# Six units of expert work ahead of a 128-step recurrence, and three in place of two between its steps

## The chip, the cores and the metric

The kernel runs on all 8 cores of one Trainium2 chip. Each core takes 2048 of the 16384 tokens and computes them from end to end; there is no exchange between cores. The time of a run is the device time of the slowest core, in microseconds (us). The profile is that of the slowest core of one execution.

## The reference

The input is normalised over its 1024 features. Two branches read the result, and both are added to the input.

```python
xn = _layernorm(x)
# branch 1: a recurrence over the tokens of a sequence
u = xn @ Wi.T + bi ; sp = xn @ Ws.T + bs        # 128 states
state = tanh(state @ A.T + u_t @ B.T) + sp_t
y_t = state @ C.T ; out1 = ys @ Wo.T + bo
# branch 2: 8 experts, the best 2 of each token, weighted
w = softmax over the top 2 of xn @ router_weight, zero elsewhere
gate, up = xn @ gate_up_proj (1024 -> 1024 each)
act = (clip(up, -7, 7) + 1) * min(gate, 7) * sigmoid(1.702 * gate)
out2 = sum_e w[e] * (act[e] @ down_proj[e])
y = x + out1 + out2
```

## The kernel before, in words

The program is written out in Python as five lists of instructions, one for each engine, in the order of the Python code. Nothing reorders them. An instruction waits on semaphore counts given where it is written; VectorE's and ScalarE's instructions also wait for the one before them on their own engine.

A core's work has four stages.

1. Normalisation of 17 blocks of 128 tokens (16 own, one of the tokens before), their transposition to `xn_fm`, the projections `u` and `sp`, the term of the recurrence that doesn't depend on the state (`Dt`), and the routing weights.
2. The recurrence, called the chain here. The 2048 tokens are cut into 64 pieces of 32; each piece starts 96 tokens early from a zero state, so that the chain has `NSTEP` = 96 + 32 = 128 steps, and each step handles one token of all 64 pieces. Step s is a matmul of `sAT` (L693, 64 columns) that adds A times the last state to a bank of PSUM, and a tanh on ScalarE (L702) that writes the new state. For each pair of steps, two matmuls of the identity (L680) first place `Dt` in the banks `pb4` and `pb5`. Steps 0 to 95 write the small buffer `gw`; steps 96 to 127 write `G`, a strided tile of which every 32nd column is written at a time. A step's matmul waits for the tanh of the step before.
3. Output of branch 1: u_bf (L712) on VectorE, a matmul by C (L721), 64 matmuls by Wo and the down bias (L736, L741) that ScalarE moves to `acc` (L746), and on VectorE 32 multiplications of expert 0's activations by their routing weights (L755).
4. The experts: down projection of expert 0 (L866, added to `acc` at L882), then gate, up and down of experts 1 to 7, and the output.

The gate and up projections of expert 0 do not wait for the chain, and are woven into it. They are 32 tiles (8 slices of 128 features, 4 of 512 tokens each), and `gu_tile_gen` writes one tile: 8 matmuls of 512 columns for gate (L277), 8 for up (L287), and then the elementwise work. The generator pauses after every second matmul, so a tile has 8 units of 2 matmuls, and all of expert 0 has 256. The elementwise work of a tile comes when the generator is resumed after its eighth unit. `pump(n)` writes the next n units, and goes from one tile to the next. For a tile of expert 0 the elementwise work is seven instructions on VectorE (casts of gate and up from PSUM, L311 and L313; L318, L321, L324; L335 and L338), and one sigmoid on ScalarE (L326), which stands in ScalarE's list between two tanhs. The sigmoid needs L318, and L335 needs the sigmoid. Gate and up use two PSUM banks each in turn, so that a tile's matmuls wait for the casts of the tile two before. After the chain, `pump_all` writes whatever units are left.

Of the kernel before, what the change touches and what calls it, by code (L numbers as in the profile page):

```python
# [35 lines left out]
def build_nc(debug=False, upto="full", ntc_run=None, skip_big=False):  # L36
# [48 lines left out]
    with ExitStack() as _es:  # L85
# [73 lines left out]
        if True:  # L159
# [48 lines left out]
            try:  # L208
# [139 lines left out]
                def pump(n):  # L348
                    k = 0
                    while k < n:  # L350
                        if pump_cur[0] is None:
                            if not pump_q:
                                return
                            ei_, fc_, stt_ = pump_q[0]
                            if stt_ > ready_st[0]:
                                return
                            pump_q.pop(0)
                            pump_cur[0] = gu_tile_gen(ei_, fc_, stt_, weighted=False)
                        try:
                            next(pump_cur[0])  # L360
                            k += 1
                        except StopIteration:
                            pump_cur[0] = None
# [300 lines left out]

                if PH < 2: raise _Done()
                ch_act = {}
                for s in range(NSTEP):
                    pump(2)
                    b = s % 2
                    if b == 0:  # L670
                        for k in range(2):
                            sk = s + k
                            if sk >= NSTEP:
                                break
                            wl = []
                            if k == 0:
                                wl = [("s_ve", ve_d_all),
                                      ("s_sc", ch_act[s - 1] if s > 0 else cnt["s_sc"])]
                            te(lambda e, sk=sk, bk=pb[4 + sk % 2]:
                               e.matmul(bk[:, 0:NCH], sI16[:],  # L680
                                        Dt[:, WOFF + sk:WOFF + sk + SSTR:LCH],
                                        start=True, stop=False, skip_group_check=True),
                               wait=wl, inc=False)
                    if s == 0:
                        rhs = gz[:]
                    elif s <= WCH:
                        rhs = gw[:, ((s - 1) % 2) * NCH:((s - 1) % 2) * NCH + NCH]
                    else:
                        t0 = s - 1 - WCH
                        rhs = G[:, t0:t0 + SSTR:LCH]  # L690
                    wl = [("s_sc", ch_act[s - 1])] if s > 0 else []
                    mv = te(lambda e, b=b, rhs=rhs:
                            e.matmul(pb[4 + b][:, 0:NCH], sAT[:], rhs,  # L693
                                     start=False, stop=True, skip_group_check=True),
                            wait=wl)
                    if s < WCH:
                        dst = gw[:, (s % 2) * NCH:(s % 2) * NCH + NCH]
                    else:
                        t0 = s - WCH
                        dst = G[:, t0:t0 + SSTR:LCH]  # L700
                    ch_act[s] = sc(lambda e, b=b, dst=dst:
                                   e.activation(dst, pb[4 + b][:, 0:NCH], ACT.Tanh),  # L702
                                   wait=[("s_te", mv)])
# [310 lines left out]
```

How the kernel before makes its waits and increments, by code:

```python
                    def op(e, fn=fn, w=w, v=v, sem_name=sem_name):  # L176
                        for sn, val in w:
                            e.wait_ge(sems[sn], val)
                        ins = fn(e)
                        if v is not None:
                            ins.then_inc(sems[sem_name], 1)
# [19 lines left out]
                def op(e, dst=dst, src=src, w=w, sem_name=sem_name):  # L201
                    for sn, val in w:
                        e.wait_ge(sems[sn], val)
                    e.dma_start(dst, src).then_inc(sems[sem_name], 16)
# [706 lines left out]
            def fin(e):  # L911
                if fin_o0:
                    e.wait_ge(s_ou0, fin_o0)
                if fin_o1:
                    e.wait_ge(s_ou1, fin_o1)
```

## Time and profile before

| | us |
|---|---|
| median of 8 runs | 1665.14 |
| lowest and highest of them | 1662.87, 1714.15 |
| the profiled execution's own time | 1663.5 |
| its span, slowest core (core 1) | 1662.0 |
| spans of the 8 cores | 1657.9 to 1662.0 |
| first gate matmul of expert 0 | 156.91 |
| last tanh of the chain begins | 316.49 |
| first u_bf addition (L712) begins | 319.84 |

Times inside the execution are counted from the span's start. The chain and expert 0's gate and up take from 156.91 to 316.49, that is, about a tenth of the span; the expert work of stage 4 fills nearly all the rest after 359.61.

### The profile page before, as it was taken

The page shows a single profiled execution, that of the slowest core. Times are in us where ns is not written, and L with a number is a line of the kernel's source. Part 1 is how long each engine was busy: PE and PEld are TensorE (multiplying, and loading weights), DVE is VectorE, ACT ScalarE, POOL GpSimd, SP SyncE. Part 2 cuts the span into 40 slices and gives each one's busy share as a digit, 9 for nine tenths or more (in the row PEclk, how much of TensorE's full clock was granted, in tenths as well). Part 3 has the DMA queues.
Part 4 walks back from the last instruction along what each step waited for, and adds up shares of the span by engine and source line. Part 5 has one row for each costly group of instructions (what it writes and reads, how often), then busy time and mean ns, then how long its engine had stood idle before and what let it go on. Part 6 is the DMA issues. An engine that isn't in the chain of part 4 may idle for free.

```text
span 1662.0 us, 25899 instructions; the slowest of 8 cores (1657.9 to 1662.0 us)
## 1 busy us (share of the span) xinstructions
PE 1485.9 (89%) x6998; PEld 669.4 (40%) x6998; DVE 903.0 (54%) x2133; ACT 560.4 (34%) x1013; POOL 120.3 (7%) x230
## 2 busy tenths in 40 slices
PE   0445888899999999999999999999999999999973
PEld 0221444324444444444444444444444444444432
DVE  4554666623566456635664466446644665366543
ACT  3442333440554045404550355025512551155200
POOL 2000000000000000000000000000000000000011
PEclk9766999869999999999999999999999999999995
DMA  5400111102222222221222222212221222222158
GB/s 145 112 26 1 27 26 27 26 7 39 33 39 40 39 31 39 39 45 26 38 40 45 33 39 39 41 30 39 39 45 27 39 39 44 33 39 39 20 113 211
DMA packets 36314, 74.66 MB, mean 45 GB/s; under 512 B 4864, under 2 KB 4864, under 8 KB 36176
## 3 DMA queue, kind: packets, MB, share of 16 engines
q0 software_dynamic: 31424, 55.71, 22.3%
q1 hardware_dynamic: 4752, 17.30, 3.1%
q8 instruction: 63, 1.03, 0.3%
q14 instruction: 75, 0.61, 0.1%
HBM read 120.10 MB, written 8.39 MB: 77 GB/s over the span
## 4 chain that ended last, share of the span: by engine, by line
PE 82%; DVE 6%; DMA 5%; ACT 3%; issue 3%; DVEq 0%; ACTq 0%; POOL 0%; POOLq 0%; SPq 0%
PE pb L287 27%; PE pb L866 26%; PE pb L277 25%; DMA y<-otm 1%; DMA xres<-xm 1%; DVE etu L313 1%; PE pb L736 1%; PE pb L741 1%; ACT et L326 1%; PE pb L479 1%; DVE acc L882 1%; DVE otm L800 1%; PE pb L693 1%; DVE etg L318 1%; PE pb L680 1%
## 5 line engine op out<-in xcount | busy, mean ns | idle before, releaser
L277 PE MATMUL pb<-xn_fm,wgu 128*128 128x512 bf16 x2048 | 496.3, 383 | 1.6 <-ACT wbc L656 1.0
L287 PE MATMUL pb<-xn_fm,wgu 128*128 128x512 bf16 x2048 | 490.4, 380 | 0.0
L866 PE MATMUL pb<-act_w,wdb_ 128*128 128x512 bf16 x2048 | 450.2, 382 | 6.8 <-DVE acc L882 5.9
L882 DVE TENSOR_TENSOR acc<-acc,pb 128x512 bf16<-128x512 bf16 x256 | 176.1, 688 | 276.5 <-PE pb L866 273.9
L866 PEld LDWEIGHTS pb<-act_w,wdb_ 128*128 128x128 bf16 x2048 | 200.9, 98 | 252.9 <-issue 16.3
L277 PEld LDWEIGHTS pb<-xn_fm,wgu 128*128 128x128 bf16 x2048 | 197.8, 99 | 239.3 <-issue 17.2
L287 PEld LDWEIGHTS pb<-xn_fm,wgu 128*128 128x128 bf16 x2048 | 197.6, 98 | 229.8 <-issue 3.3
L307 ACT CAST etu<-pb 128x512 bf16<-128x512 f32 x224 | 131.3, 586 | 256.0 <-PE pb L287 256.0
L326 ACT ACTIVATE et<-etg 128x512 bf16<-128x512 bf16 x256 | 161.1, 629 | 66.4 <-DVE etg L318 32.4
L305 ACT CAST etg<-pb 128x512 bf16<-128x512 f32 x224 | 131.3, 586 | 91.1 <-PE pb L277 90.3
L321 DVE TENSOR_SCALAR etu<-etu,sbu 128x512 bf16<-128x512 bf16 x256 | 91.9, 359 | 110.5 <-ACT etu L307 104.9
L839 ACT CAST wbc<-pb 128x512 bf16<-128x512 f32 x28 | 16.4, 586 | 394.8 <-PE pb L833 392.8
L318 DVE TENSOR_SCALAR etg<-etg,sbg 128x512 bf16<-128x512 bf16 x256 | 90.4, 353 | 81.7 <-DVE act_w L338 38.2
L331 DVE TENSOR_TENSOR et2w<-et,wbc 128x512 bf16<-128x512 bf16 x224 | 95.2, 425 | 54.5 <-DVE etu L324 53.1
L338 DVE TENSOR_TENSOR act_w<-etu,et2w 128x512 bf16<-128x512 bf16 x256 | 108.8, 425 | 26.7
L333 DVE TENSOR_TENSOR et2w<-etg,et2w 128x512 bf16<-128x512 bf16 x224 | 95.3, 426 | 23.3
L204 POOL DMA_DIRECT2D wgu<-Wg x64 | 33.9, 529 | 778.3 <-PE pb L287 546.5
L324 DVE TENSOR_SCALAR etu<-etu 128x512 bf16<-128x512 bf16 x256 | 75.4, 295 | 27.2
L204 POOL DMA_DIRECT2D wdb_<-Wd x64 | 33.8, 528 | 442.2 <-PE pb L866 398.0
L204 POOL DMA_DIRECT2D wgu<-Wu x64 | 34.3, 537 | 235.6 <-DMA wgu<-Wg 214.5
L702 ACT ACTIVATE gw<-pb 128x64 bf16<-128x64 f32 x96 | 21.5, 224 | 57.8 <-PE pb L693 54.4
L313 DVE CAST etu<-pb 128x512 bf16<-128x512 f32 x32 | 22.1, 692 | 25.8 <-PE pb L693 25.8
(105 smaller groups left out, 515.7 us busy)
## 6 DMA issues: line engine op xcount, KB each, us to landing
wgu<-Wg POOLq DMA_DIRECT2D x64, 256.0 KB, 3.5
wgu<-Wu POOLq DMA_DIRECT2D x64, 256.0 KB, 3.6
wdb_<-Wd POOLq DMA_DIRECT2D x64, 256.0 KB, 3.5
xln<-xm SPq DMA_DIRECT2D x16, 512.0 KB, 4.1
y<-otm SPq DMA_DIRECT2D x16, 512.0 KB, 5.7
xres<-xm POOLq DMA_DIRECT2D x16, 256.0 KB, 6.7
xln<-xw SPq DMA_DIRECT2D x1, 512.0 KB, 5.4
sWiT<-WiT POOLq DMA_DIRECT2D x1, 256.0 KB, 6.6
```

Of the source, the lines that this page charges most:

```text
L204: e.dma_start(dst, src).then_inc(sems[sem_name], 16)
L277: e.matmul(bg_[:, 0:STW], wgu[:, 2 * par, dc, :], rhs, start=(dc == 0), stop=(dc == NDC - 1)),
L287: e.matmul(bu2[:, 0:STW], wgu[:, 2 * par + 1, dc, :], rhs, start=(dc == 0), stop=(dc == NDC - 1)),
L305: cg = sc(lambda e, tg=tg, bg_=bg_: e.copy(tg, bg_[:, 0:STW]), wait=[("s_te", mg)])
L307: cu = sc(lambda e, tu=tu, bu2=bu2: e.copy(tu, bu2[:, 0:STW]), wait=[("s_te", mu2)])
L318: e.tensor_scalar(t1, tg, gbias, LIMIT, ALU.add, ALU.min),
L326: e.activation(t2, t1, ACT.Sigmoid, scale=ALPHA),
L331: e.tensor_mul(t2w, t2, wbs),
L333: ve(lambda e, t3=t3, t1=t1, t2w=t2w: e.tensor_mul(t3, t1, t2w))
L338: e.tensor_mul(act_w[:, fc, stt * STW:(stt + 1) * STW], t5_, t3))
L866: e.matmul(bk[:, 0:STW], wdb_[:, par, ic, :], act_w[:, ic, stt * STW:(stt + 1) * STW], start=(ic == 0), stop=(ic == NDC - 1), skip_group_c ...
L882: e.tensor_add(acc[:, fc, stt * STW:(stt + 1) * STW], acc[:, fc, stt * STW:(stt + 1) * STW], bk[:, 0:STW]),
```

## The change

Six units of expert 0 are written ahead of step 0, and each step is preceded by three units in place of two.

```diff
                 ch_act = {}
+                pump(6)
                 for s in range(NSTEP):
-                    pump(2)
+                    pump(3)
                     b = s % 2
```

Before, 128 steps of 2 units made the 256 units. Now 6 + 3 x 83 = 255 units stand ahead of step 83, the last one is written by step 83's call, and steps 84 to 127 have no expert work among them. All lines below the change are one number higher in the new kernel: L680, L693, L702, L712, L736, L866 become L681, L694, L703, L713, L737, L867.

The first place is the start of the chain on TensorE. In these rows `pb_43` and `pb_44` are the two gate banks, `pb_45` and `pb_46` the two up banks, `pb_47` and `pb_48` the two banks of the chain. Before:

```order
L650 MATMUL pb_46<-w_fmb,ssel 128x512
L277 MATMUL pb_43<-xn_fm,wgu 128x512 x4
L680 MATMUL pb_47<-Dt,sI 128x64
L680 MATMUL pb_48<-Dt,sI 128x64
L693 MATMUL pb_47<-gz,sAT 128x64
L277 MATMUL pb_43<-xn_fm,wgu 128x512 x4
L693 MATMUL pb_48<-gw,sAT 128x64
L287 MATMUL pb_45<-xn_fm,wgu 128x512 x4
```

And now:

```order
L650 MATMUL pb_46<-w_fmb,ssel 128x512
L277 MATMUL pb_43<-xn_fm,wgu 128x512 x8
L287 MATMUL pb_45<-xn_fm,wgu 128x512 x8
L277 MATMUL pb_44<-xn_fm,wgu 128x512 x2
L681 MATMUL pb_47<-Dt,sI 128x64
L681 MATMUL pb_48<-Dt,sI 128x64
L694 MATMUL pb_47<-gz,sAT 128x64
L277 MATMUL pb_44<-xn_fm,wgu 128x512 x6
L694 MATMUL pb_48<-gw,sAT 128x64
L287 MATMUL pb_46<-xn_fm,wgu 128x512 x6
```

The whole first tile and a unit of the second now stand ahead of step 0, and six matmuls of 512 columns stand between two chain matmuls.

The second place is ScalarE's list between two sigmoids, in the first part of the chain. Before, a sigmoid stands after every four tanhs:

```order
L326 ACTIVATE et2<-etg 128x512
L702 ACTIVATE gw<-pb4_47 128x64
L702 ACTIVATE gw<-pb5_48 128x64
L702 ACTIVATE gw<-pb4_47 128x64
L702 ACTIVATE gw<-pb5_48 128x64
L326 ACTIVATE et2<-etg 128x512
```

And now:

```order
L326 ACTIVATE et2<-etg 128x512
L703 ACTIVATE gw<-pb5_48 128x64
L703 ACTIVATE gw<-pb4_47 128x64
L703 ACTIVATE gw<-pb5_48 128x64
L326 ACTIVATE et2<-etg 128x512
L703 ACTIVATE gw<-pb4_47 128x64
L703 ACTIVATE gw<-pb5_48 128x64
L326 ACTIVATE et2<-etg 128x512
```

Three, three and two tanhs stand between sigmoids now, over and over.

The third place is on TensorE where the expert work ends. Before, it ends with the chain:

```order
L693 MATMUL pb4_47<-G,sAT 128x64
L287 MATMUL pb3_46<-xn_fm,wgu 128x512 x4
L693 MATMUL pb5_48<-G,sAT 128x64
L721 MATMUL pb4_47<-u_bf,sCT 128x512
```

And now, at steps 83 to 85:

```order
L287 MATMUL pb3_46<-xn_fm,wgu 128x512 x2
L694 MATMUL pb5_48<-gw,sAT 128x64
L681 MATMUL pb4_47<-Dt,sI16 128x64
L681 MATMUL pb5_48<-Dt,sI16 128x64
L694 MATMUL pb4_47<-gw,sAT 128x64
L694 MATMUL pb5_48<-gw,sAT 128x64
```

After the last unit, only chain matmuls of 64 columns follow, up to step 127.

## Rows read from the trace of the kernel before

**Rows 1.** The groups of tanhs: count, busy us, mean ns, idle before and releaser.
```profile
L702 ACT ACTIVATE gw<-pb 128x64 bf16<-128x64 f32 x96 | 21.5, 224 | 57.8 <-PE pb L693 54.4
L702 ACT ACTIVATE G<-pb 128x64 bf16<-128x64 f32 x32 | 14.5, 452 | 15.5 <-PE pb L693 14.3
```

**Rows 2.** Stretches: us, each engine's busy us (count), granted clock, DMA share, GB/s.
```profile
160.00:162.00 2.00, 2.00 (x7) 0.77 (x6) 0.69 (x1) 0.22 (x1) 0.00 (x0) 0.51 0.00 0
324.00:358.00 34.00, 33.75 (x63) 6.31 (x63) 11.95 (x29) 20.90 (x31) 0.00 (x0) 0.50 0.00 0
110.00:120.00 10.00, 2.73 (x32) 2.14 (x32) 6.38 (x23) 4.05 (x8) 0.00 (x0) 0.54 0.00 1
160.00:270.00 110.00, 99.11 (x544) 47.83 (x543) 71.86 (x155) 34.03 (x112) 5.28 (x10) 0.99 0.16 25
```

**Rows 3.** Waits from 157 to 317: total us, times, longest.
```profile
ACT et L326 <- DVE etg L318: 31.6, 31, 1.4
PE pb L693 <- ACT gw L702: 11.4, 23, 0.8
```

**Rows 4.** Timeline of one tile's loop: start, length, engine, line, idle before.
```profile
202.38 0.69 DVE L313 CAST etu<-pb 128x512 bf16<-128x512 f32 x1 [0.69 <-PE pb L693]
203.25 0.35 DVE L318 TENSOR_SCALAR etg<-etg,sbg 128x512 bf16<-128x512 bf16 x1 [0.18 <-DVE etu L313]
203.69 0.63 ACT L326 ACTIVATE et<-etg 128x512 bf16<-128x512 bf16 x1 [1.06 <-DVE etg L318]
204.47 0.22 ACT L702 ACTIVATE gw<-pb 128x64 bf16<-128x64 f32 x1
204.84 0.19 PE L693 MATMUL pb<-gw,sAT 128*128 128x64 bf16 x1 [0.49 <-ACT gw L702]
204.96 1.02 PE L287 MATMUL pb<-xn_fm,wgu 128*128 128x512 bf16 x4
205.12 0.22 ACT L702 ACTIVATE gw<-pb 128x64 bf16<-128x64 f32 x1 [0.43 <-PE pb L693]
205.23 0.43 DVE L338 TENSOR_TENSOR act_w<-etu,et2w 128x512 bf16<-128x512 bf16 x1
205.82 0.38 PE L680 MATMUL pb<-Dt,sI 128*128 128x64 bf16 x2
205.83 0.69 DVE L311 CAST etg<-pb 128x512 bf16<-128x512 f32 x1 [0.17 <-DVE act_w L338]
206.03 0.21 PE L693 MATMUL pb<-gw,sAT 128*128 128x64 bf16 x1
206.07 1.02 PE L287 MATMUL pb<-xn_fm,wgu 128*128 128x512 bf16 x4
207.20 0.69 DVE L313 CAST etu<-pb 128x512 bf16<-128x512 f32 x1 [0.69 <-PE pb L693]
208.07 0.35 DVE L318 TENSOR_SCALAR etg<-etg,sbg 128x512 bf16<-128x512 bf16 x1 [0.18 <-DVE etu L313]
```

**Rows 5.** Timeline of the chain's first step.
```profile
156.91 1.86 PE L277 MATMUL pb<-xn_fm,wgu 128*128 128x512 bf16 x4 [1.03 <-ACT wbc L656]
158.80 0.23 PE L693 MATMUL pb<-gz,sAT 128*128 128x64 bf16 x1
159.13 0.22 ACT L702 ACTIVATE gw<-pb 128x64 bf16<-128x64 f32 x1 [2.57 <-PE pb L693]
```

**Rows 6.** Timeline in the last quarter: tanh to matmul to tanh.
```profile
308.22 0.45 ACT L702 ACTIVATE G<-pb 128x64 bf16<-128x64 f32 x1
308.81 0.27 PE L693 MATMUL pb<-G,sAT 128*128 128x64 bf16 x1 [0.76 <-ACT G L702]
309.18 0.45 ACT L702 ACTIVATE G<-pb 128x64 bf16<-128x64 f32 x1 [0.51 <-PE pb L693]
```

**Rows 7.** Timeline at the chain's end: the last tanh and the first addition after it.
```profile
316.49 0.45 ACT L702 ACTIVATE G<-pb 128x64 bf16<-128x64 f32 x1 [0.52 <-PE pb L693]
319.84 2.02 DVE L712 TENSOR_TENSOR u_bf<-G,SPb 128x512 bf16<-128x512 bf16 x4 [0.17 <-DVE act_w L338]
```

## The prediction, made before the changed kernel ran

> **What bounds the kernel now.** I read the page's 40 slices first: TensorE is busy through the chain and through the experts, so only one stretch can be moved by this change, that from the first gate matmul at 156.91 [rows 5] to the first u_bf addition at 319.84 [rows 7]. All later stages start from that addition. So the forecast is the new time of that addition, less 319.84.
>
> TensorE's busy share in that stretch looks like a bound (99.1 of 110 us), but busy time of pipelined matmuls overstates it. The waits say otherwise: the sigmoid waited 31 times for VectorE's L318, 31.6 us in all, and a chain matmul waited 23 times for its tanh in the first 96 steps [rows 3]. So I followed one tile in the timeline [rows 4]. L318 begins at 203.25, the sigmoid that it releases at 203.69, the tanh queued behind the sigmoid at 204.47, the chain matmul that waits for that tanh at 204.84. Only then does TensorE go on: four matmuls of 512 columns from 204.96, the pair of L680 at 205.82, the next chain matmul at 206.03, four more from 206.07. The last four end the up projection of the tile; VectorE's cast of it starts at 207.20, and L318 of the next tile at 208.07. This is a closed loop of 208.07 - 203.25 = 4.82 us a tile: 1.59 us from L318 to the chain matmul, 2.36 from there to the up cast, 0.87 from cast to L318. Neither engine fills it. Free of waits, TensorE would need per tile 16 matmuls of 0.215 us (four take 205.82 - 204.96 = 0.86), that is 3.44, and for four steps 4 x 0.11 + 2 x 0.21 = 0.86, together 4.3. VectorE needs 205.83 - 203.25 = 2.58 from L318 to the next gate cast, and 0.87 each for the two casts (each is a cast of 0.69 and a gap near 0.18, as from 202.38 to 203.25), together 4.32.
>
> **The first three quarters of the units, faster.** In the new order (the order of the two kernels is in the section on the change) 3 units stand between chain matmuls, so a tile spans 8/3 steps. TensorE's floor falls to 3.44 + 8/3 x 0.11 + 4/3 x 0.21 = 4.0 us; VectorE's stays at 4.32. The loop depends on how many units of tile n+1 come ahead of the chain matmul that is held by tile n's sigmoid. Before, these were always 4, and 4 were left. Now it is 4, then 6, then 5, in turn, as the 3, 3, 2 tanhs between sigmoids tell. With 4 ahead the loop stays as it was, 4 units left and about 4.82. With 5 or 6 ahead, 3 or 2 units are left: 1.59 + 0.12 + 3 x 0.43 + 0.27 = 3.27 us from L318 until the up cast can start (0.27 is the delay from TensorE's end to the cast, 207.20 less 206.07 + 0.86), while VectorE itself is ready for that cast only after 2.58 + 0.87 = 3.45. So there VectorE is the bound and a tile takes 4.32. Mean (4.82 + 2 x 4.32)/3 = 4.49.
>
> The head: the first tile's 16 matmuls now run without a chain step among them. The granted clock was 0.51 up to 162 [rows 2], which is 1.2 GHz, and 512 columns take 0.427 there: four of them lasted 1.86, the last one's drain included [rows 5]. From 156.91 to 161.9 these are 11.7 matmuls, the other 4.3 take 0.9: tile 0 is through at 162.8, and its L318 begins at 162.8 + 0.27 + 0.87 = 164.0. Then 31 loops, 11 of 4.82 and 20 of 4.32, are 139.4 us: the last tile's L318 begins at 303.4. The sigmoid of this tile is written ahead of step 83's tanh, so the matmul of step 84 comes 1.59 later, plus the pair of L680 ahead of it: 305.1. Before, by the same measure, 2 units a step carried the expert work to the end of the chain.
>
> **The last 44 steps, bare.** From step 84 nothing is left to weave in, and a step costs its latency. In the first kind of step (gw) the tanh's start to the next chain matmul is 204.84 - 204.47 = 0.37, the matmul to its tanh 205.12 - 204.84 = 0.28 [rows 4]: 0.65 us, and 0.21 more where a pair of L680 comes in between (205.82 to 206.03): 0.86. For steps that write G the two are 308.81 - 308.22 = 0.59 and 309.18 - 308.81 = 0.37 [rows 6], so 0.96, and 1.17 with a pair; half of this is the tanh itself, 0.452 us against 0.224 [rows 1]. Twelve gw steps: 6 x 0.65 + 6 x 0.86 = 9.1. From step 96 to step 127's matmul: 16 x 0.96 + 15 x 1.17 = 32.9, and 0.37 + 0.45 to the end of its tanh. Sum 42.8 us at full clock.
>
> The clock will not be full. Where TensorE was busy 2.73 of 10 us, the granted clock was 0.54 [rows 2], that is, mostly 1.2 GHz, and in the bare steps TensorE has a matmul of 64 columns or three of them in about 1 us. At that level step 0 had 0.33 from matmul to tanh [rows 5] against 0.28. No row shows the other side, tanh to matmul, or a pair of L680 that has waited, at that level; I take 0.07 us more per step in all, between 0 and 0.15. So 44 x 0.07 = 3.1, and the tail is 45.9 us (42.8 to 49.4). The Trainium skill says in "TensorE: Matmul & The Clock Gate", section "The HAM clock gate", that half rate is the default and that activity releases it; by that rule the tail is at 1.2 GHz throughout. By the page's formulas for a single matmul (section "Single matmul latency") 64 columns would take an estimated 236 ns there and 193 ns at 2.4 GHz, and the tail would grow by 44 x 0.04 = 1.9 us, and by more where a pair precedes; by "no change of clock" it would be 42.8. The trace's step 0 agrees in direction with the page (0.33 against 0.28), and no row here shows a run of bare steps.
>
> **Sum.** End of the last tanh 305.1 + 45.9 = 351.0. VectorE has by then long finished the last tile (before, that tile held the u_bf addition until 319.84, nearly 3 us after the tanh's end at 316.94; this wait of 2.9 us goes and is in the sum), so the addition starts 0.2 later, at 351.2. Against 319.84 that is +31.4 us. The rest costs nothing new: the same output stage and the same experts follow. Weight loads of expert 0 have 4 tiles, 17 to 19 us, per slice for two transfers of 3.5 us each, and those of expert 1 are issued earlier; the L755 multiplications still lie under the output stage, which ran at a clock of 0.50 before [rows 2] and starts from a slow clock again. The profiled execution took 1663.5, so it would take 1694.9; the median before is 1.6 above it, so I expect 1696.5 as a median, 1.9% slower. (A difference of under 0.2% could not be told from none.)
>
> **Rivals.**
>
> A. *The tile loop does not shorten.* If something puts the slow case in every tile (VectorE held by a sigmoid that comes later, say), 31 loops of 4.82 are 149.4, 10.0 us more: +41.4, 1706. For it speaks that the waits [rows 3] are the same every tile; against it, that in two of three tiles fewer units are left behind the held matmul.
>
> B. *Handoffs in the tail are cheap.* If the gaps around a tanh were due to the 512-column matmuls in TensorE's queue, and went away when it is empty, a step would cost its tanh and the matmul's issue: 12 x 0.25 + 32 x 0.48 = 18.4 us in place of 45.9. That alone leaves +3.9. Together with the same gap gone from the slow tile loops (each at VectorE's 4.32, 5.5 us less) the addition would come at 318.2, 1.6 us sooner than before: 1663.5 as a median, on the faster side of nothing. It decides at 44 steps in 14.5 us, 0.33 each, for the tail alone, less than the mean tanh of 0.39 [rows 1]. And the matmul at 204.84 found TensorE idle for 0.49 us [rows 4]: nothing was ahead of it in the queue, and it still came 0.37 after its tanh's start. So there is next to nothing for it.
>
> C. *The clock rises in the output stage.* It stood at 0.50 for 34 us although TensorE was busy 33.75 of them [rows 2]. If the other history brought it to full there, ScalarE's 32 moves, 0.69 and a gap near 0.1 each, would set the pace: 25.3 in place of 34, so +31.4 - 8.7 = +22.7, 1688. The stage begins after a low clock in both kernels, so little speaks for it.
>
> D. *The change leaves the order as it was.* Excluded by the order of instructions, where steps 84 to 127 stand bare.
>
> **How the numbers follow.** Forecast 0.82 (its own range 1692 to 1702, from the tail's 42.8 to 49.4 and 2 us on the loops), A 0.09, C 0.06, B 0.01, other 0.02. The range from 1689 to 1703 leaves out most of A and C. Slower by over 0.2%: all but B and a part of "other", 0.98; within 0.2%: 0.01; faster: 0.01.
>
> **What would show it.** In the profile after: L318 starts of neighbouring tiles 4.3, 4.3 and 4.8 us apart up to about 303; the last gate or up matmul near 302; from there to about 351 TensorE with a low busy share and a clock near 0.5, chain matmuls 0.7 to 0.95 us apart up to step 96 and 1.0 to 1.25 after it; VectorE idle for 45 us; u_bf's addition at 351; the stages behind it shifted as a block by 31. The forecast is wrong if tiles come under 4.2 or all over 4.7 us apart, if tail steps take under 0.9 or over 1.15 us in the mean, or if a stage behind 351 is longer or shorter by over 2 us.

## The result, and the profile after

The changed kernel takes 1694.9 us (median of 11 runs) against 1665.07 (31 runs): a ratio of 1.0182, with a 95% interval of 1.0173 to 1.0191. Some executions of either kernel were several per cent longer, with one half of the chip at a lower granted clock; the medians here count them, all the ratios leave them out. The change makes the kernel 1.8% slower. The profiled execution took 1694.22; its slowest core, core 5, spans 1692.7.

Here is where the chain's stretch begins and ends in each execution, for the slowest core. The two last rows take out that cores reach the chain at slightly different times.

| us | before (core 1) | changed (core 5) |
|---|---|---|
| first gate matmul | 156.91 | 157.69 |
| last tile's L318 | 317.26 | 306.41 |
| last tanh ends | 316.94 | 351.43 |
| first u_bf addition | 319.84 | 351.53 |
| from the first gate matmul to that addition | 162.9 | 193.8 |
| from that addition to the span's end | 1342.2 | 1341.2 |

The loss is the 30.9 us of the second last row. All that follows has kept its length within 1 us. The other cores say the same: over all eight, the stretch of the second last row is 162.9 to 163.2 us before and 193.4 to 193.8 now, and the rest takes 1340.8 in the mean before and 1340.3 now.

In the timeline of the changed kernel the columns are start, length, engine, line, operation, and in brackets the idle time before with its releaser. Here are two tiles in a row, each from one L318 on VectorE to the next, with the lines that matter for them (others between are left out):

```profile
202.58 0.35 DVE L318 TENSOR_SCALAR etg<-etg,sbg 128x512 bf16<-128x512 bf16 x1 [0.18 <-DVE etu L313]
204.27 0.19 PE L694 MATMUL pb<-gw,sAT 128*128 128x64 bf16 x1
206.03 0.69 DVE L313 CAST etu<-pb 128x512 bf16<-128x512 f32 x1 [0.17 <-PE pb L694]
206.90 0.35 DVE L318 TENSOR_SCALAR etg<-etg,sbg 128x512 bf16<-128x512 bf16 x1 [0.17 <-DVE etu L313]
207.34 0.63 ACT L326 ACTIVATE et<-etg 128x512 bf16<-128x512 bf16 x1 [2.56 <-DVE etg L318]
208.12 0.23 ACT L703 ACTIVATE gw<-pb 128x64 bf16<-128x64 f32 x1
208.49 0.19 PE L694 MATMUL pb<-gw,sAT 128*128 128x64 bf16 x1 [1.19 <-ACT gw L703]
208.62 1.46 PE L287 MATMUL pb<-xn_fm,wgu 128*128 128x512 bf16 x6
210.86 0.69 DVE L313 CAST etu<-pb 128x512 bf16<-128x512 f32 x1 [0.69 <-PE pb L287]
211.72 0.35 DVE L318 TENSOR_SCALAR etg<-etg,sbg 128x512 bf16<-128x512 bf16 x1 [0.18 <-DVE etu L313]
```

From 202.58 to 206.90 a tile took 4.32 us, and the up cast at 206.03 began as soon as VectorE was free (0.17, its usual gap). From 206.90 to 211.72 it took 4.82: the chain matmul at 208.49 had waited for the tanh at 208.12, which stood behind the sigmoid at 207.34; it came 1.59 us after L318, as in [rows 4], and the up cast at 210.86 had to wait 0.69 for TensorE. Over the chain the L318s come about 4.31, 4.31 and 4.83 us apart in turn.

The tail, where nothing is woven in, first in gw steps and then in G steps:

```profile
311.09 0.38 PE L681 MATMUL pb<-Dt,sI 128*128 128x64 bf16 x2 [0.47 <-ACT gw L703]
311.30 0.23 PE L694 MATMUL pb<-gw,sAT 128*128 128x64 bf16 x1
311.62 0.23 ACT L703 ACTIVATE gw<-pb 128x64 bf16<-128x64 f32 x1 [0.68 <-PE pb L694]
311.99 0.21 PE L694 MATMUL pb<-gw,sAT 128*128 128x64 bf16 x1 [0.47 <-ACT gw L703]
312.30 0.23 ACT L703 ACTIVATE gw<-pb 128x64 bf16<-128x64 f32 x1 [0.45 <-PE pb L694]
312.67 0.38 PE L681 MATMUL pb<-Dt,sI 128*128 128x64 bf16 x2 [0.47 <-ACT gw L703]
312.88 0.23 PE L694 MATMUL pb<-gw,sAT 128*128 128x64 bf16 x1
...
345.37 0.29 PE L694 MATMUL pb<-G,sAT 128*128 128x64 bf16 x1
345.76 0.45 ACT L703 ACTIVATE G<-pb 128x64 bf16<-128x64 f32 x1 [0.73 <-PE pb L694]
346.35 0.27 PE L694 MATMUL pb<-G,sAT 128*128 128x64 bf16 x1 [0.69 <-ACT G L703]
346.71 0.45 ACT L703 ACTIVATE G<-pb 128x64 bf16<-128x64 f32 x1 [0.51 <-PE pb L694]
347.31 0.38 PE L681 MATMUL pb<-Dt,sI 128*128 128x64 bf16 x2 [0.69 <-ACT G L703]
347.51 0.29 PE L694 MATMUL pb<-G,sAT 128*128 128x64 bf16 x1
```

Two gw steps take 312.88 - 311.30 = 1.58 us, two G steps 347.51 - 345.37 = 2.14. TensorE waits for ScalarE at each step and ScalarE for TensorE. The stretches of the same execution (columns as in [rows 2]) give the clock in the tail and in the output stage, and the waits from 157 to 352 (total us, times, longest) what VectorE does meanwhile:

```profile
320.00:345.00 25.00, 8.64 (x45) 3.96 (x45) 0.00 (x0) 10.74 (x24) 0.00 (x0) 0.50 0.00 1
356.00:389.00 33.00, 32.86 (x62) 6.10 (x61) 11.74 (x28) 20.65 (x30) 0.00 (x0) 0.50 0.00 0
```

```profile
DVE u_bf L713 <- ACT G L703: 42.7, 1, 42.7
```

In the tail the granted clock is 0.50, the lower level of 1.2 GHz, and VectorE stands idle for 42.7 us. And at the head, step 0 shows a wait that was not there before:

```profile
165.48 0.63 ACT L326 ACTIVATE et<-etg 128x512 bf16<-128x512 bf16 x1 [8.15 <-DVE etg L318]
166.26 0.38 PE L681 MATMUL pb<-Dt,sI 128*128 128x64 bf16 x2 [1.77 <-ACT et L326]
166.46 0.21 PE L694 MATMUL pb<-gz,sAT 128*128 128x64 bf16 x1
```

Step 0's first matmul waits for the last ScalarE instruction written so far (`cnt["s_sc"]`). Nine units are written ahead of it now, the six and step 0's own three, so the first tile's elementwise work is too, and that last instruction is the first tile's sigmoid. TensorE idles 1.77 us.

### The profile page after: what moved, and what is told of

It reads as the page before. It is cut to its first block, busy times and chain, and to the rows that moved or that the text cites. A ratio compares the mean times of both kernels' runs of the same rounds, so it can differ in the third digit from the quotient of the medians.

```text
span 1692.7 us, 25899 instructions; the slowest of 8 cores (1687.9 to 1692.7 us)
## 1 busy us (share of the span) xinstructions
PE 1488.9 (88%) x6998; PEld 669.9 (40%) x6998; DVE 903.1 (53%) x2133; ACT 561.4 (33%) x1013; POOL 120.4 (7%) x230
## 4 chain that ended last, share of the span: by engine, by line
PE 83%; DVE 5%; DMA 4%; ACT 4%; issue 3%; DVEq 0%; ACTq 0%; POOL 0%; POOLq 0%; SPq 0%
PE pb L287 26%; PE pb L867 26%; PE pb L277 25%; DMA xres<-xm 2%; PE pb L681 1%; PE pb L737 1%; PE pb L742 1%; DVE etu L313 1%; ACT G L703 1%; PE pb L479 1%; ACT et L326 1%; PE pb L694 1%; DVE acc L883 1%; DVE otm L801 1%; PE pb L491 1%
## 5 line engine op out<-in xcount | busy, mean ns | idle before, releaser
L867 PE MATMUL pb<-act_w,wdb_ 128*128 128x512 bf16 x2048 | 449.7, 382 | 6.8 <-DVE acc L883 5.9
L867 PEld LDWEIGHTS pb<-act_w,wdb_ 128*128 128x128 bf16 x2048 | 200.9, 98 | 252.8 <-issue 16.2
L318 DVE TENSOR_SCALAR etg<-etg,sbg 128x512 bf16<-128x512 bf16 x256 | 90.5, 354 | 81.4 <-DVE act_w L338 38.2
L338 DVE TENSOR_TENSOR act_w<-etu,et2w 128x512 bf16<-128x512 bf16 x256 | 108.8, 425 | 26.7
L204 POOL DMA_DIRECT2D wgu<-Wu x64 | 34.0, 531 | 259.5 <-DMA wgu<-Wg 191.0
L681 PE MATMUL pb<-Dt,sI 128*128 128x64 bf16 x128 | 24.3, 278 | 21.1 <-ACT G L703 10.3
L703 ACT ACTIVATE gw<-pb 128x64 bf16<-128x64 f32 x96 | 21.6, 225 | 55.8 <-PE pb L694 51.3
```

Source lines behind the costliest of these rows:

```text
L204: e.dma_start(dst, src).then_inc(sems[sem_name], 16)
L338: e.tensor_mul(act_w[:, fc, stt * STW:(stt + 1) * STW], t5_, t3))
L867: e.matmul(bk[:, 0:STW], wdb_[:, par, ic, :], act_w[:, ic, stt * STW:(stt + 1) * STW], start=(ic == 0), stop=(ic == NDC - 1), skip_group_c ...
```

## Experiments

The theory T: the change splits the chain into 84 steps paced by the tiles (4.31 us, every third 4.83, for 8/3 steps) and 44 bare steps that cost their handoffs, and the second part is far dearer than what the first gives back. Each time below is a median with its ratio to the kernel before on the same chip; "stretch" is the time from the first gate matmul to the first u_bf addition on the slowest core of the profiled execution (162.9 before, 193.8 changed). Bare steps are those with no expert work among them, and the tail is the run of bare steps at the chain's end.

**Three units, none ahead.**

```diff
-                    pump(2)
+                    pump(3)
```

> Three units before each step, no six ahead: one part of the change alone. Theory T (the loss is the bare tail, priced by its own latency): units end in step 85, so 42 bare steps in place of 44, two gw steps fewer (2 x 0.79 = 1.6 us), and step 0 no longer waits for the first tile's sigmoid (1.1 us in the profile of the changed kernel). Expect about 2.5 us less than the changed kernel: 1692 to 1693, ratio to before 1.0165. Rival R1 (the six units ahead, a head of TensorE work that delays the chain, carry a good part of the loss): then this kernel should be at least 6 us below the changed one, 1689 or less.

Measured: 1691.53 us, ratio 1.0170 (1.0154 to 1.0186); stretch 191.0, which is 2.9 less than the changed kernel's. The number of units a step carries the loss; R1, the head, falls.

**Six units ahead, two a step.**

```diff
+                pump(6)
                 for s in range(NSTEP):
                     pump(2)
```

> Six units ahead, two before each step: the other part alone. Theory T: units end in step 124 and only three steps are bare; the tile loops stay at 4.83 us. The last tile's L318 comes near 316.9 as before, and three bare G steps with their last tanh follow: +1 us (0 to 2), 1666, no difference that this measurement tells well. Rival R1: the head costs by itself, 5 us or more, 1670 and above.

Measured: 1663.83 us, ratio 1.0003 (0.9992 to 1.0014); stretch 162.1. That is 0.9 less than before where I expected 1 more. The tile loops in the gw part are mostly 4.73 to 4.82, a little under the 4.83 of before, which I put down to the pair of L681 standing elsewhere in the tile (not tried); and the addition no longer waits for the last tile. No difference in time, as expected.

**The bare steps first.**

```diff
-                    pump(2)
+                    pump(3 if s >= 42 else 0)
```

> No units before steps 0 to 41, three before each of steps 42 to 127: as many bare steps as with three only (42), but at the chain's start, where each writes gw, while the 32 G steps have expert work among them. Theory T (a bare step costs its handoffs, 0.79 us in the mean for gw and 1.07 for G): the bare part is 42 x 0.79 = 33 us in place of 43, the G steps under expert work add about 0.3 us to each slow tile only, and the last tile's work on VectorE holds the u_bf addition by 2 us again. u_bf addition near 341.7, about +22 on before: 1686 to 1688. Rival R2 (bare steps cost by their number, not by kind, or the start of the clock from rest costs as much again): the same as three only, within 2 us, 1692.

Measured: 1684.13 us, ratio 1.0124 (1.0108 to 1.0140); stretch 184.1, here from step 0's first L680 at 157.34, as no gate matmul stands ahead of it, to 341.46 (expected 341.7). The median is 2 us under the 1686 to 1688 expected; by the ratio the kernel is 20.6 us above the kernel before, where that forecast means 21 to 23. With the same 42 bare steps this is 7.4 us under the first experiment by the medians, and 6.9 by the stretches. Its bare steps, in the timeline:

```profile
187.77 0.23 PE L693 MATMUL pb<-gw,sAT 128*128 128x64 bf16 x1
188.09 0.22 ACT L702 ACTIVATE gw<-pb 128x64 bf16<-128x64 f32 x1 [0.67 <-PE pb L693]
188.46 0.21 PE L693 MATMUL pb<-gw,sAT 128*128 128x64 bf16 x1 [0.47 <-ACT gw L702]
188.77 0.22 ACT L702 ACTIVATE gw<-pb 128x64 bf16<-128x64 f32 x1 [0.45 <-PE pb L693]
189.14 0.38 PE L680 MATMUL pb<-Dt,sI 128*128 128x64 bf16 x2 [0.47 <-ACT gw L702]
189.34 0.23 PE L693 MATMUL pb<-gw,sAT 128*128 128x64 bf16 x1
```

189.34 - 187.77 = 1.57 for two steps, as the 1.58 in the changed kernel's gw tail, where two G steps took 2.14. A bare step is priced by its kind, and the dear G steps are the ones to hide. R2 falls.

**TensorE kept busy in the tail.** The changed kernel with two extra matmuls of 512 columns before each bare step. They write bank `pb[0]`, which is not read again before it is overwritten.

```diff
                 for s in range(NSTEP):
+                    if not pump_q and pump_cur[0] is None:
+                        for k in range(2):
+                            te(lambda e: e.matmul(pb[0][:, 0:STW], sAT[:],
+                                                  xn_fm[:, WC:WC + 4, 0, :],
+                                                  start=True, stop=True),
+                               wait=[ts_read[0][0]], inc=False)
                     pump(3)
```

> The changed kernel with two extra matmuls of 512 columns before each bare step, that write a bank nobody reads afterwards; they keep TensorE busy and fit into the waits (0.43 us at 2.4 GHz beside a step of 0.65 or more). Theory T (the tail is ScalarE and handoff latency, and the clock has almost no part in it): granted clock 1.0 in the tail, tail shorter by 0.5 us or equal, 1694 to 1695; if the clock stayed low the two would take 0.85 us and the tail would grow by 5 to 12 us. Rival R3 (the half-rate clock costs 0.07 us a step, as the prediction took it): 3 us less than the changed kernel, 1692. Rival C of the prediction (a different history brings the output stage to full clock): 8 to 9 us less, 1686, with a granted clock of 1.0 behind the tail.

Measured: 1693.76 us, ratio 1.0181 (1.0159 to 1.0202); stretch 193.9, against 193.8. The stretches of this kernel, early in the tail, further on, and in the output stage:

```profile
308.00:309.00 1.00, 1.00 (x7) 0.45 (x5) 0.00 (x0) 0.22 (x1) 0.33 (x1) 0.50 0.04 2
320.00:345.00 25.00, 19.42 (x94) 8.16 (x91) 0.00 (x0) 10.75 (x24) 0.00 (x0) 1.00 0.01 1
356.00:389.00 33.00, 32.07 (x61) 5.99 (x61) 10.00 (x24) 21.07 (x31) 0.00 (x0) 0.50 0.00 0
```

And two of its G steps, at full clock:

```profile
332.53 0.29 PE L700 MATMUL pb<-G,sAT 128*128 128x64 bf16 x1
332.92 0.45 ACT L709 ACTIVATE G<-pb 128x64 bf16<-128x64 f32 x1 [0.73 <-PE pb L700]
333.51 0.27 PE L700 MATMUL pb<-G,sAT 128*128 128x64 bf16 x1 [0.26 <-ACT G L709]
333.88 0.45 ACT L709 ACTIVATE G<-pb 128x64 bf16<-128x64 f32 x1 [0.51 <-PE pb L700]
334.47 0.38 PE L687 MATMUL pb<-Dt,sI 128*128 128x64 bf16 x2 [0.24 <-ACT G L709]
334.67 0.29 PE L700 MATMUL pb<-G,sAT 128*128 128x64 bf16 x1
```

The clock went from 0.50 to 1.00 and two G steps still take 334.67 - 332.53 = 2.14. The extra matmuls do not hide a gain: the G step's matmul at 333.51 found TensorE idle for 0.26 us. In the 25 us from 320 to 345 ScalarE does 24 tanhs either way. R3 falls.

The equal stretch is in part a balance. The clock fell in this kernel too, after TensorE had idled 1.73 us up to 305.36, and was low from about 307.3 to 310.7. There the extra matmuls stood in the way, and two pairs of steps took 1.89 and 1.96 us in place of 1.53: the 12 gw steps took 10.0 us, against 9.4 in the changed kernel. The 31 steps behind them took 32.9, against 33.0.

The output stage is at 0.50 here as well. The clock had fallen again by 352, after TensorE was busy 1.15 of the 3 us from 349, so the stage did not begin at full clock; but it stayed at 0.50 through 33 us of which TensorE was busy 32.07. The 8 to 9 us of rival C did not come.

**The sigmoid after the next tanh.** This and the next two test the tile loop. In the kernel before, for expert 0 only; `rest` writes the sigmoid, L335 and L338, and `later` is emptied behind the tanh of each step and once behind `pump_all`:

```diff
-                    sg = sc(lambda e, t2=t2, t1=t1:
-                            e.activation(t2, t1, ACT.Sigmoid, scale=ALPHA),
-                            wait=[("s_ve", vg)])
+                    if not weighted:
+                        later.append(rest)
+                        return
...
                                    wait=[("s_te", mv)])
+                    while later:
+                        later.pop(0)()
```

> The kernel before (two units a step, none ahead), with one thing moved: a tile's sigmoid, and the two VectorE multiplications behind it, are written after the next tanh instead of before it. Theory L (each tile is a closed loop because a tanh stands behind a sigmoid that waits for VectorE's L318): the loop of 4.83 us opens, a tile falls to the floor of TensorE and VectorE, 4.3 to 4.4, in the G steps too, where it was 5.13: 24 x 0.5 + 8 x 0.75 = 18 us less, 1647, ratio 0.989. Rival V (VectorE and TensorE together need what they take, and the order on ScalarE is nothing): within 0.2% of before.

VectorE's order stays as it was, L335 and L338 in front of the next tile's casts, so only ScalarE's order is changed.

Measured: 1649.77 us, ratio 0.9916 (0.9897 to 0.9936), where 1647 and 0.989 were expected; stretch 148.8, 14.1 less than before. One of its tiles (L327 is the sigmoid, L707 the chain matmul, L716 the tanh):

```profile
203.94 0.22 ACT L716 ACTIVATE gw<-pb 128x64 bf16<-128x64 f32 x1 [0.95 <-PE pb L707]
204.07 0.35 DVE L318 TENSOR_SCALAR etg<-etg,sbg 128x512 bf16<-128x512 bf16 x1 [0.18 <-DVE etu L313]
204.52 0.63 ACT L327 ACTIVATE et<-etg 128x512 bf16<-128x512 bf16 x1 [0.36 <-DVE etg L318]
204.54 0.19 PE L707 MATMUL pb<-gw,sAT 128*128 128x64 bf16 x1
206.66 0.69 DVE L311 CAST etg<-pb 128x512 bf16<-128x512 f32 x1 [0.17 <-DVE act_w L336]
207.52 0.69 DVE L313 CAST etu<-pb 128x512 bf16<-128x512 f32 x1 [0.17 <-DVE etg L311]
208.39 0.35 DVE L318 TENSOR_SCALAR etg<-etg,sbg 128x512 bf16<-128x512 bf16 x1 [0.17 <-DVE etu L313]
```

The chain matmul at 204.54 no longer waits, both casts start right behind VectorE's last work, and a tile takes 208.39 - 204.07 = 4.32, VectorE's own time. That is so for all but two of the gw tiles. In the G steps a tile takes 4.59 to 5.30, mostly near 4.95, where I had expected about 4.35: there a tanh of 0.45 runs ahead of the sigmoid, which starts 1.24 us after L318 (0.45 in the gw tile above), and VectorE waits 0.69 for it. Theory L holds in the gw steps, V falls, and the size for the G steps was wrong. This version beats both kernels.

**The same in the changed kernel.** The same edit on top of the change.

> The changed kernel with the sigmoid moved in the same way. Theory L: only every third tile was slow there (4.83 against VectorE's 4.31), so 11 x 0.5 = 5.5 us go, and 1.1 at step 0, whose first matmul no longer waits for the first sigmoid. The bare tail of 43 us stays. 6 to 7 us less than the changed kernel: 1688, ratio 1.014. Rival V: 1694. If the gain is as large as in the kernel before (18 us, 1677), the loop was wrongly read as closed in only one tile of three.

Measured: 1687.41 us, ratio 1.0146 (1.0129 to 1.0164), 7.5 less than the changed kernel's median, and 6.0 less by the two ratios; stretch 185.9, 7.9 less. Its tiles are 4.30 to 4.32 us apart but for two of 4.66. Of the 7.9, 7.1 are in the 31 tile loops: the slow tile in three and the wait at step 0. The other 0.9 are behind the last L318, where the last sigmoid no longer stands ahead of a tanh.

**Step 0 without the first tile's sigmoid.** The edit is made in the changed kernel. `bc0_done` is the count of the last ScalarE instruction ahead of the chain.

```diff
-                                      ("s_sc", ch_act[s - 1] if s > 0 else cnt["s_sc"])]
+                                      ("s_sc", ch_act[s - 1] if s > 0 else bc0_done)]
```

> The changed kernel, where the first matmul of step 0 waits for the last ScalarE instruction ahead of the chain instead of the last one written so far, which is now the first tile's sigmoid. Theory T: TensorE's idle of 1.8 us ahead of step 0 goes, the second tile comes about 4.8 us after the first in place of 5.9, and the end of the chain comes 1.1 us sooner after the first gate matmul: 1693 to 1694. Rival: the second tile's lateness is the slow clock of the head; then its 5.9 us stay.

Measured: 1694.61 us (two runs), ratio 1.0188 (1.0163 to 1.0212), which can't tell 1 us. Its profile can: the first two L318s are 4.73 us apart in place of 5.91, TensorE has no idle before step 0, and the stretch is 192.6, 1.3 less.

## Why the prediction was right, point by point

The time was 1694.9, predicted 1696.5, and the profiled execution 1694.2 against 1694.9. That the sum is nearly exact is luck: the steps up to the tail came out 2.3 us longer than predicted and the tail 2.7 shorter. Either error alone would have stayed inside the forecast's range of 1692 to 1702. By its steps, on the slowest cores:

| step | predicted us | measured us |
|---|---|---|
| first gate matmul to the first L318 | 7.1 | 7.3 |
| 31 tile loops | 139.4 | 141.4 |
| last L318 to step 84's matmul | 1.7 | 1.8 |
| tail to the end of the last tanh | 45.9 | 43.2 |
| to the u_bf addition | 0.2 | 0.1 |

The third row's own terms, 1.59 and 0.21 for the pair, make 1.8, as measured; the sum in the prediction took 1.7.

*The bound before was a closed loop of 4.82 us, not TensorE.* Shown by moving one sigmoid: the loop opened and gave 14 us of the stretch back with the same instructions and the same order on VectorE and TensorE, though TensorE had read 90% busy [rows 2].

*A tile takes 4.31, 4.31, 4.82 in turn.* Right, in the timeline above and in the 7.9 us of the change with the sigmoid moved. The 2.0 us that the sum of loops missed have a place. 1.1 are the new wait at step 0 (its loop took 5.91), which I failed to see: the change wrote the first tile ahead of a wait that says "the last instruction so far". The experiment on it took this away. Another 0.7 are two loops of 4.66 for 4.31, the second and the last but two, where VectorE's gap before L318 is 0.35 longer; such a longer gap is there in all the kernels, before too, and what makes it stays open. The rest is a few slow loops of 4.89.

*The tail is latency.* Right: 12 gw steps took 317.62 - 308.21 = 9.4 us (9.1 predicted at full clock), the next 31 to step 127's matmul 33.0 (32.9). The handoffs read from single waits before [rows 4, 6] hold within 0.04 us for 44 steps in a row. Rival B, that they would vanish with an empty queue, is refuted by the same rows.

*The slow clock adds 3.1 us.* Wrong in size. The clock did fall to 0.50, but the G steps take 2.14 a pair at either level, and the gw steps 1.58 against 1.53 (309.74 - 308.21 for the changed kernel's first pair, before its clock fell, and 307.09 - 305.56 in the kernel with the filled tail), so it costs about 0.3 us in the whole tail. The 0.07 us a step that the prediction took was 0.03 in the gw steps and nothing in the G steps. In the tail the Trainium skill's rule that half rate is the state without activity ("TensorE: Matmul & The Clock Gate", section "The HAM clock gate") agrees with the trace: the clock was 0.50 with TensorE busy 8.64 of 25 us. The output stage does not fit that rule, with 0.50 and TensorE busy 32.86 of 33 us. Of the 43 ns more that the Trainium skill's formulas for a single matmul give for 64 columns (an estimate, same page, section "Single matmul latency"), 0.03 us is seen in the gw steps between a matmul and the tanh that it releases, 0.31 for 0.28; the G steps show nothing, 0.36 to 0.39 at either level.

*Rivals.* A (all loops slow) is refuted by the L318s, C (the output stage at full clock) by 0.50 there in both kernels, and in the kernel whose tail ran mostly at full clock too. *The rest of the program unchanged:* 1341.2 against 1342.2.

The trade is then plain. Before, 128 steps took 159.6 us with the expert work nearly free. Now 84 steps carry that work, and its last L318 comes 11.6 us sooner after the first gate matmul; then 44 steps cost 43 us, in which VectorE idles and TensorE and ScalarE mostly wait for each other.

## What to carry to other kernels

When independent work is woven into a latency chain, its amount per step has to last to the chain's end: a bare step costs its full handoffs, so front-loading pays a latency for each step that it lays bare, and if some must be bare, let it be the cheap ones. Before adding work per step, follow one round of the loop: here the step was held by a tanh queued behind a sigmoid that waited for a third engine, and moving that sigmoid by one place gained 0.84%, where adding work lost 1.8%. A wait written as "everything issued so far" changes its meaning when code is put ahead of it.

## What the hardware showed that I had not expected

- The matmul-to-tanh-to-matmul handoff hardly depends on TensorE's clock: a pair of G steps took 2.14 us at a granted clock of 0.50 and of 1.00, a pair of gw steps 1.58 and 1.53. That holds for a chain alone: where two matmuls of 512 columns stood before each step, a pair of gw steps took up to 1.96 at the low clock.
- A matmul of 64 columns that reads the strided `G` and a tanh that writes it cost 0.37 to the tanh and 0.59 back, against 0.28 and 0.37 for the small packed buffer; 0.23 of this is the tanh itself (0.452 against 0.224), and what makes the other 0.08, the strided access or something that goes with it, was not measured apart.
- The output stage stayed at a clock of 0.50 with TensorE busy 32.86 of 33 us, and 32.07 when most of the tail in front of it had run at 1.00. What keeps it there was not tried; its matmuls alternate between 128 and 8 rows.
